# A sequence's routing laid out in six steps of a common clock instead of four, in a fused two-layer decoder kernel

## The chip, the cores and the metric

The kernel runs on one core of a Trainium2 chip. The metric is the device time of one execution in microseconds (us). Before the change it is 425.02 us, the median of 3 runs that lie between 424.5 and 425.11. The engines are named as in the profile: PE is the matrix engine (TensorE), PEld its weight loads, DVE the vector engine, ACT the scalar engine, POOL the GpSimd engine, SP the engine that here only issues DMAs.

## What is computed

The reference takes 4 sequences of 256 tokens of width 128 through two decoder layers. Each layer is self attention, cross attention and a mixture of 8 experts, with a layer norm behind each. The last of these, the second layer's mixture, sends every token to one expert with room for 128 tokens. What the change touches is how a token gets its place there (`_L1_ffn_ref`, cut):

```python
probs = jax.nn.softmax(xf.astype(jnp.float32) @ Wr, axis=-1)
eidx = jnp.argmax(probs, axis=-1)
p_tok = jnp.take_along_axis(probs, eidx[:, None], axis=1)[:, 0]
onehot = jax.nn.one_hot(eidx, E, dtype=jnp.int32)
rank_all = jnp.cumsum(onehot, axis=0) - onehot
rank = jnp.take_along_axis(rank_all, eidx[:, None], axis=1)[:, 0]
keep = rank < cap
slot = jnp.where(keep, rank, cap)
...
xe = xf[dispatch]
h = jnp.maximum(jnp.einsum('ecd,edf->ecf', xe, W1), 0.0)
ye = jnp.einsum('ecf,efd->ecd', h, W2)
```

## The kernel before, in words

Each engine has one program, written out in full before the launch. Its order comes from a clock that all engines' programs share: `by_the_clock` starts the stages (attention of a sequence, mixture, causal attention, routing) at given ticks and, in every tick, calls each live stage once, the one that started earliest first. What a stage emits in its step s stands in tick start + s, on every engine. Within an engine the instructions then run strictly in that order. Semaphores hold an instruction back until what it reads is there, and everything behind it on its engine waits too.

An attention takes 16 heads through these steps: from step 0 a head's scores by query go to a bank of pool D (L709) and DVE takes the row maxima (L1250, `negmax`); after each four heads two transposes (`shift`, L693) bring the maxima back and DVE adds them to the queries (L1245, `q_sp`); from step 8 a head's scores by key go to pool A (L720) and ACT takes exponentials (L997, `expo`); at steps 17 and 25 come the weighted values of eight heads each, into the one bank of pool C (L737, called pv below, `pair_done` at its end), which ACT copies out (L1003, `ctx_sb`). A mixture's products are L867 to L869 (up) and L851 (down), with DVE's L1309 behind each down product. Pool D has 4 banks and pool A 3. Banks are handed out in the order of the program, round the pool (`bank_turns`), so a product waits until the bank's last user has been read.

The routing of a sequence starts when its last attention (CROSS1) has ended, at ticks 175, 199, 223 and 239 for sequences 0 to 3. In the first three cases the attentions of later sequences are live; in the fourth nothing else is. In step 0 PE computes the logits (L919), and DVE copies them and makes the choice of the expert, the one-hot rows and their running count (L1366 to L1385, eleven small instructions, each linked to the next by a semaphore). In step 1 ACT takes the exponential (L1070) and DVE the sum (L1389 to L1391). In step 2 PE multiplies for the rank (L929, L931; needs `onehot_ready`) and DVE computes the slot (L1396 to L1404). POOL then writes the token rows to `xe_scratch` with two indirect DMAs (L515). For sequence 0 it also makes a table with an iota (L521). POOL's own list follows the order in which banks are handed out: the residual sum `xb` of an attention (L495) stands where its head 15 has its maxima, the scatter where the routing has its rank.

Before some of the last attention's products PE runs products that nobody reads (L629, `keep_busy`). After the routing of sequence 3 comes the second layer's mixture of all sequences (L1558 to L1586) and the output.

## Time and profile before

| | |
|---|---|
| median of 3 runs | 425.02 us |
| profiled execution, its own time | 425.88 us |
| span in that execution (first to last instruction) | 424.1 us |
| mean granted TensorE clock | 0.977 |
| PE busy / DVE / ACT / POOL | 377.5 / 284.7 / 226.1 / 54.4 us |
| routing of sequence 0, 1, 2, 3: logits copied by DVE at | 318.3, 350.8, 376.1, 391.8 us |

Times inside the execution count from the first instruction. Busy time says how long an engine worked, not whether anybody waited for it; for that one reads the rows in order of time, in which a bracket names the idle time of the engine before the instruction and what ended it. Matmuls overlap, so the start of the next one, not the printed end, shows when PE was ready for more.

### The profile page before, as it was taken

The page shows a single profiled execution, that of the slowest core. Times are in us where ns is not written, and L with a number is a line of the kernel's source. Part 1 is how long each engine was busy: PE and PEld are TensorE (multiplying, and loading weights), DVE is VectorE, ACT ScalarE, POOL GpSimd, SP SyncE. Part 2 cuts the span into 40 slices and gives each one's busy share as a digit, 9 for nine tenths or more (in the row PEclk, how much of TensorE's full clock was granted, in tenths as well). Part 3 has the DMA queues.
Part 4 walks back from the last instruction along what each step waited for, and adds up shares of the span by engine and source line. Part 5 has one row for each costly group of instructions (what it writes and reads, how often), then busy time and mean ns, then how long its engine had stood idle before and what let it go on. Part 6 is the DMA issues. An engine that isn't in the chain of part 4 may idle for free.

```text
span 424.1 us, 9115 instructions
## 1 busy us (share of the span) xinstructions
PE 377.5 (89%) x3274; PEld 331.8 (78%) x3274; DVE 284.7 (67%) x840; ACT 226.1 (53%) x526; POOL 54.4 (13%) x62
## 2 busy tenths in 40 slices
PE   4688898998989999999978999899999969979791
PEld 3576777886769997889967899878998757867691
DVE  6598889888965557722697264754668588853853
ACT  2145566665666564767337564585465635651241
POOL 7700004900000000000000000000003002010124
PEclk9989999999999999999979999999999989999997
DMA  5656310213340000200020000200003021652221
GB/s 157 197 160 191 113 52 26 75 47 90 123 145 2 2 2 0 76 2 2 2 68 8 2 0 2 56 21 1 2 5 85 5 71 39 204 169 63 55 69 34
DMA packets 23643, 25.68 MB, mean 61 GB/s; under 512 B 3240, under 2 KB 18353, under 8 KB 23600
## 3 DMA queue, kind: packets, MB, share of 16 engines
q1 hardware_dynamic: 22128, 23.47, 18.8%
q0 software_dynamic: 512, 0.97, 0.7%
q10 hardware_dynamic: 960, 0.66, 0.6%
q8 instruction: 27, 0.44, 0.4%
q14 instruction: 16, 0.13, 0.1%
HBM read 18.35 MB, written 6.83 MB: 59 GB/s over the span
## 4 chain that ended last, share of the span: by engine, by line
PE 68%; DVE 21%; issue 5%; ACT 3%; DMA 2%; POOLq 0%; SPq 0%; POOL 0%; ACTq 0%; DVEq 0%
PE bank_D L851 13%; PE bank_C L737 10%; PE bank_D L709 9%; PE bank_A L720 8%; DVE negmax L1250 5%; PE bank_A L867 4%; PE bank_A L869 3%; PE bank_A L868 3%; PE bank_D L635 2%; PE bank_D L693 2%; DVE x_rows L1182 1%; PE bank_D L768 1%; PE bank_A L655 1%; PE bank_A L1586 1%; PE bank_D L751 1%
## 5 line engine op out<-in xcount | busy, mean ns | idle before, releaser
L1250 DVE TENSOR_REDUCE negmax<-bank_D 128x2 f32<-128x512 f32 x192 | 127.6, 686 | 42.3 <-PE bank_D L709 41.8
L997 ACT ACTIVATE expo<-bank_A 128x512 f32<-128x512 f32 x192 | 110.2, 597 | 49.5 <-PE bank_A L720 47.2
L709 PE MATMUL bank_D<-k_head,q_sp 128*128 128x256 f32 x384 | 90.8, 321 | 9.6 <-DVE negmax L1250 4.7
L720 PE MATMUL bank_A<-q_sp,k_head 128*128 128x256 f32 x384 | 82.4, 300 | 4.9 <-DVE q_sp L1245 3.4
L1033 ACT ACTIVATE hidden<-bank_A,b 128x256 f32<-128x256 f32 x128 | 53.7, 471 | 52.1 <-PE bank_A L869 52.0
L709 PEld LDWEIGHTS bank_D<-k_head,q_sp 128*128 128x128 f32 x384 | 61.5, 199 | 21.9 <-issue 9.9
L851 PE MATMUL bank_D<-mix_w,hidden 128*128 128x128 f32 x512 | 67.8, 275 | 0.0
L720 PEld LDWEIGHTS bank_A<-q_sp,k_head 128*128 128x128 f32 x384 | 60.7, 194 | 7.7 <-DVE q_sp L1245 5.0
L851 PEld LDWEIGHTS bank_D<-mix_w,hidden 128*128 128x128 f32 x512 | 62.5, 191 | 1.6 <-issue 1.6
L737 PE MATMUL bank_C<-expo,v_aug 128*32 128x256 f32 x768 | 46.4, 382 | 1.1 <-ACT expo L997 0.5
L1309 DVE SCALAR_TENSOR_TENSOR y_mixture<-bank_D,g_w,y_mixture 128x128 f32<-128x128 f32 x64 | 22.3, 349 | 30.5 <-PE bank_D L851 28.8
L867 PE MATMUL bank_A<-x_hi,w_hi 128*128 128x256 f32 x128 | 41.2, 322 | 0.2 <-ACT hidden L1033 0.2
L495 POOL TENSOR_TENSOR xb<-x_rows,rows 128x256 f32<-128x256 f32 x12 | 8.3, 689 | 239.0 <-DVE y_attention L1230 237.4
L737 PEld LDWEIGHTS bank_C<-expo,v_aug 128*32 128x32 f32 x768 | 23.2, 109 | 16.2 <-issue 1.9
L869 PE MATMUL bank_A<-x_hi,w_lo 128*128 128x256 f32 x128 | 35.8, 279 | 0.0
L868 PE MATMUL bank_A<-x_lo,w_hi 128*128 128x256 f32 x128 | 35.7, 279 | 0.0
L1245 DVE TENSOR_TENSOR q_sp<-q_sp,bank_D 128x256 fp32r<-128x256 f32 x48 | 19.7, 410 | 8.6 <-PE bank_D L693 8.5
L867 PEld LDWEIGHTS bank_A<-x_hi,w_hi 128*128 128x128 f32 x128 | 24.3, 190 | 1.2 <-issue 0.7
L1003 ACT ACTIVATE ctx_sb<-bank_C 128x256 f32<-128x256 f32 x24 | 9.2, 385 | 28.2 <-PE bank_C L737 28.1
L868 PEld LDWEIGHTS bank_A<-x_lo,w_hi 128*128 128x128 f32 x128 | 24.3, 190 | 0.0
L869 PEld LDWEIGHTS bank_A<-x_hi,w_lo 128*128 128x128 f32 x128 | 24.1, 188 | 0.0
L515 POOL DMA_INDIRECT xe_scratch<-x_rows,slot x8 | 8.1, 1006 | 107.4 <-DVE slot L1404 106.2
(188 smaller groups left out, 529.9 us busy)
## 6 DMA issues: line engine op xcount, KB each, us to landing
mix_w<-in_mix_w SPq DMA_DIRECT2D x24, 256.0 KB, 3.5
k_head<-k_scratch SPq DMA_DIRECT2D x92, 48.0 KB
k_scratch<-qk_hi SPq DMA_DIRECT2D x24, 128.0 KB, 2.4
w_last<-in_mix_w SPq DMA_DIRECT2D x8, 256.0 KB, 6.3
k_scratch<-qk_lo SPq DMA_DIRECT2D x12, 128.0 KB, 2.3
proj_w<-in_proj SPq DMA_DIRECT2D x1, 640.0 KB, 5.7
xe_scratch<-empty_row SPq DMA_DIRECT2D x1, 520.0 KB, 4.5
expo<-xe_scratch SPq DMA_DIRECT2D x2, 260.0 KB, 3.2
```

What stands on the lines that cost most here:

```text
L709: last = mm(where(seq, b, ("max", k))[:, qt * SEQ:(qt + 1) * SEQ], q_sps[SET[seq, b]][:, k // 4, qt * P:(qt + 1) * P], k_heads[SET[seq, b] ...
L720: last = mm(where(seq, b, ("exp", h))[:, kt * SEQ:(kt + 1) * SEQ], k_heads[SET[seq, b]][:, t, g, kt * P:(kt + 1) * P], q_sps[SET[seq, b]][ ...
L737: last = mm(where(seq, b, ("pv", pair))[32 * g:32 * g + 32, 0:SEQ], v_augs[SET[seq, b]][:, kt, head(t, g), :], expo[:, exp_slot(seq, b, 4 ...
L851: last = mm(where(seq, b, ("down", e, qt))[:, 0:P], hidden[:, (e % 2) * FC + f, qt * P:(qt + 1) * P], mix_w2[:, e, f, :], start=(f == 0), ...
L867: mm(dst, w_hi, x_hi[:], start=True, stop=False)
L868: mm(dst, w_hi, x_lo[:], start=False, stop=False)
L869: last = mm(dst, w_lo, x_hi[:], start=False, stop=True)
L997: activate(expo[:, exp_slot(seq, b, h), :], where(seq, b, ("exp", h))[:], ACT.Exp, scale=float(HD) ** -0.5).then_inc(free(seq, b, ("exp", ...
L1033: last = activate(hidden[:, (e % 2) * FC + f, :], where(seq, b, ("up", n))[:, i * SEQ:(i + 1) * SEQ], ACT.Relu, bias=b1[:, e * FC + f:e * ...
L1245: V.tensor_tensor(q_sp[:, t, :], q_sp[:, t, :].bitcast(f32), where(seq, b, ("shift", t))[:, 0:SEQ], ALU.add).then_inc(free(seq, b, ("shift ...
L1250: V.tensor_reduce(negmaxes[SET[seq, b]][:, s // 4, :, 32 * (s % 4)], where(seq, b, ("max", s))[:].rearrange("p (q n) -> p q n", q=QT), AX. ...
L1309: V.scalar_tensor_tensor(y[b][:, qt, :], where(seq, b, ("down", e, qt))[:, 0:P], g_w[:, qt, e:e + 1], y[b][:, qt, :], ALU.mult, ALU.add).t ...
```

## The change

The routing gets six steps, with names. Logits on PE stay in step 0. DVE's choice moves from step 0 to step 1, ACT's exponential from 1 to 2, DVE's sum from 1 to 3, PE's rank product from 2 to 4, and DVE's slot from 2 to 5. No instruction is added or removed, and the starting ticks of all stages stay.

```diff
-ROUTE_STEPS = range(4)
+LOGITS_AT, FLAGS_AT, ROUTE_EXP_AT, TOTAL_AT, RANK_AT, SLOT_AT = 0, 1, 2, 3, 4, 5
+ROUTE_STEPS = range(SLOT_AT + 1)
...
     def routing(seq, b):
         for s in ROUTE_STEPS:
-            if s == 0:
+            if s == LOGITS_AT:
                 turn(seq, b, "logits", "D")
-            if s == 2:
+            if s == RANK_AT:
                 turn(seq, b, "rank", "D")
             yield
...
-                        if s == 2:
+                        if s == RANK_AT:
                             wait_free(pe, seq, b, "rank")
                             keep_busy(seq, b, where(seq, b, "rank"), "rank")
                             pe.wait_ge(onehot_ready, seq + 1)
...
-                        if s == 1:
+                        if s == ROUTE_EXP_AT:
                             act.wait_ge(shifted, seq + 1)
...
+                    for _ in range(FLAGS_AT):
+                        yield
+
                     wait_filled(dve, seq, ROUTE, "logits")
...
-                    yield
+                    for _ in range(FLAGS_AT, TOTAL_AT):
+                        yield
 
                     dve.wait_ge(routeexp_ready, seq + 1)
...
-                    yield
+                    for _ in range(TOTAL_AT, SLOT_AT):
+                        yield
```

The new lines shift the line numbers: PE's by 1, DVE's below the routing's choice by 4 to 6. In the rows below, L720 before is L721 of the change, L929 is L930, and so on.

Place 1 is the routing of sequence 0. This is PE's program there before the change, from the logits to pv of heads 0 to 7 of sequence 1:

```order
L919 MATMUL bank_D<-gate_w,xT_all 128x8 x2
L709 MATMUL bank_D<-k_head,q_sp 128x256 x2
L720 MATMUL bank_A<-q_sp,k_head 128x256 x2
L851 MATMUL bank_D<-mix_w,hidden 128x128 x4
L709 MATMUL bank_D<-k_head,q_sp 128x256 x2
L720 MATMUL bank_A<-q_sp,k_head 128x256 x2
L851 MATMUL bank_D<-mix_w,hidden 128x128 x4
L929 MATMUL bank_D<-onehot,const 128x8
L931 MATMUL bank_D<-before,const 128x8
L929 MATMUL bank_D<-onehot,const 128x8
L931 MATMUL bank_D<-before,const 128x8
```

And this is PE's program of the change, from the second of these two down products on, up to pv:

```order
L852 MATMUL bank_D<-mix_w,hidden 128x128 x4
L694 MATMUL bank_D<-const,negmax 128x128 x2
L710 MATMUL bank_D<-k_head,q_sp 128x256 x2
L721 MATMUL bank_A<-q_sp,k_head 128x256 x2
L852 MATMUL bank_D<-mix_w,hidden 128x128 x4
L710 MATMUL bank_D<-k_head,q_sp 128x256 x2
L721 MATMUL bank_A<-q_sp,k_head 128x256 x2
L930 MATMUL bank_D<-onehot,const 128x8
L932 MATMUL bank_D<-before,const 128x8
L930 MATMUL bank_D<-onehot,const 128x8
L932 MATMUL bank_D<-before,const 128x8
L721 MATMUL bank_A<-q_sp,k_head 128x256 x4
```

The rank's four products stood ahead of the shift (L693), head 14's scores, head 6's exponentials, a down product and heads 15 and 7; now they stand behind them, ahead of heads 8 and 9.

On DVE, at the same place, this stood between the end of the choice (L1385) and the slot before the change:

```order
L1385 TENSOR_REDUCE route_col<-route 128x2
L1250 TENSOR_REDUCE negmax<-bank_D 128x2
L1309 SCALAR_TENSOR_TENSOR y_mixture<-bank_D,g_w,y_mixture 128x128
L1389 TENSOR_REDUCE route_col<-route 128x2
L1390 RECIPROCAL x_rows<-route_col 128x2
L1391 COPY x_rows<-const 128x2
L1250 TENSOR_REDUCE negmax<-bank_D 128x2
L1309 SCALAR_TENSOR_TENSOR y_mixture<-bank_D,g_w,y_mixture 128x128
L1396 TENSOR_TENSOR route<-bank_D,onehot 128x16
```

In the change the choice ends with L1389, and this follows it:

```order
L1389 TENSOR_REDUCE route_col<-route 128x2
L1251 TENSOR_REDUCE negmax<-bank_D 128x2
L1310 SCALAR_TENSOR_TENSOR y_mixture<-bank_D,g_w,y_mixture 128x128
L1246 TENSOR_TENSOR q_sp<-q_sp,bank_D 128x256
L1251 TENSOR_REDUCE negmax<-bank_D 128x2
L1310 SCALAR_TENSOR_TENSOR y_mixture<-bank_D,g_w,y_mixture 128x128
L1394 TENSOR_REDUCE route_col<-route 128x2
L1395 RECIPROCAL x_rows<-route_col 128x2
L1396 COPY x_rows<-const 128x2
L1251 TENSOR_REDUCE negmax<-bank_D 128x2
L1168 BN_STATS stats_mixture<-y_mixture 128x6 x2
L1171 BN_AGGR mv_mixture<-stats_mixture 128x2 x2
```

One maximum (head 12) and one down product's sum that stood behind the choice now stand ahead of it, so what follows it is head 13 and the down product after.

Place 3 is the routing of sequence 2. PE's program there before, from the logits to the products that nobody reads ahead of the last pv:

```order
L919 MATMUL bank_D<-gate_w,xT_all 128x8 x2
L720 MATMUL bank_A<-q_sp,k_head 128x256 x4
L929 MATMUL bank_D<-onehot,const 128x8
L931 MATMUL bank_D<-before,const 128x8
L929 MATMUL bank_D<-onehot,const 128x8
L931 MATMUL bank_D<-before,const 128x8
L720 MATMUL bank_A<-q_sp,k_head 128x256 x4
L629 MATMUL bank_C<-proj_w 128x128 x4
```

And in the change:

```order
L920 MATMUL bank_D<-gate_w,xT_all 128x8 x2
L721 MATMUL bank_A<-q_sp,k_head 128x256 x8
L930 MATMUL bank_D<-onehot,const 128x8
L932 MATMUL bank_D<-before,const 128x8
L930 MATMUL bank_D<-onehot,const 128x8
L932 MATMUL bank_D<-before,const 128x8
L630 MATMUL bank_C<-proj_w 128x128 x4
```

The scores of heads 14 and 15 have moved from behind the rank to ahead of it. POOL's list changes at two places: the residual sums of sequence 1 and of sequence 2 stood behind the scatters of sequence 0 and of sequence 1, and now stand ahead of them. At the routing of sequence 3 every engine's order is the same as before.

## Rows read from the trace of the kernel before

**Rows 1.** The page: each engine's busy time, share and instructions.
```profile
PE 377.5 (89%) x3274; PEld 331.8 (78%) x3274; DVE 284.7 (67%) x840; ACT 226.1 (53%) x526; POOL 54.4 (13%) x62
```

**Rows 2.** PE in order of time, place 1: start, duration, instruction [idle before].
```profile
318.71 1.05 PE L851 MATMUL bank_D<-mix_w,hidden 128*128 128x128 f32 x8
320.08 1.05 PE L851 MATMUL bank_D<-mix_w,hidden 128*128 128x128 f32 x8
...
324.00 0.88 PE L720 MATMUL bank_A<-q_sp,k_head 128*128 128x256 f32 x6
325.18 1.93 PE L737 MATMUL bank_C<-expo,v_aug 128*32 128x256 f32 x32 [0.30 <-issue]
...
328.66 0.41 PE L779 MATMUL bank_A<-const,x_rows 128*128 128x128 f32 x2 [0.28 <-DVE x_rows L1182]
```

**Rows 3.** DVE in order of time, place 1.
```profile
318.33 0.18 DVE L1366 COPY route<-bank_D 128x16 f32<-128x16 f32 x1 [0.37 <-PE bank_D L919]
...
320.36 0.68 DVE L1250 TENSOR_REDUCE negmax<-bank_D 128x2 f32<-128x512 f32 x1
320.96 0.34 DVE L1309 SCALAR_TENSOR_TENSOR y_mixture<-bank_D,g_w,y_mixture 128x128 f32<-128x128 f32 x1
...
326.57 0.65 DVE L1179 SCALAR_TENSOR_TENSOR newton_mixture<-newton_mixture,r_mixture 128x2 f32<-128x2 f32 x1
327.25 0.62 DVE L1180 SCALAR_TENSOR_TENSOR newton_mixture<-newton_mixture,r_mixture 128x2 f32<-128x2 f32 x1
```

**Rows 4.** DVE's line L1179 over the whole execution: count, minimum, median, maximum ns.
```profile
L1179 DVE SCALAR_TENSOR_TENSOR newton_mixture<-newton_mixture,r_mixture x4: 160/163/646, 170.6 to 326.6; 128x2 f32<-128x2 f32 x4
```

**Rows 5.** POOL in order of time, scatters of sequences 0 to 2, the iota, a residual sum.
```profile
324.19 1.15 POOL L515 DMA_INDIRECT xe_scratch<-x_rows,slot  x1 [54.97 <-DVE slot L1404]
...
326.61 0.59 POOL L521 IOTA rope<- 128x512 f32 x1
327.14 0.71 POOL L495 TENSOR_TENSOR xb<-x_rows,rows 128x256 f32<-128x256 f32 x1
356.38 0.99 POOL L515 DMA_INDIRECT xe_scratch<-x_rows,slot  x1 [28.54 <-DVE slot L1404]
357.68 0.97 POOL L515 DMA_INDIRECT xe_scratch<-x_rows,slot  x1 [0.30 <-issue]
...
381.97 0.97 POOL L515 DMA_INDIRECT xe_scratch<-x_rows,slot  x1 [0.31 <-issue]
```

**Rows 6.** ACT in order of time, places 1 and 2.
```profile
327.17 0.39 ACT L1003 ACTIVATE ctx_sb<-bank_C 128x256 f32<-128x256 f32 x1 [0.41 <-PE bank_C L737]
...
330.31 0.38 ACT L966 ACTIVATE aT_causal<-bank_A 128x256 f32<-128x256 f32 x1 [0.28 <-PE bank_A L881]
...
359.24 0.38 ACT L1003 ACTIVATE ctx_sb<-bank_C 128x256 f32<-128x256 f32 x1 [1.68 <-PE bank_C L737]
```

**Rows 7.** PE in order of time, place 2 (the routing of sequence 1).
```profile
352.87 0.28 PE L929 MATMUL bank_D<-onehot,const 128*128 128x8 f32 x2
...
355.94 0.50 PE L720 MATMUL bank_A<-q_sp,k_head 128*128 128x256 f32 x2 [0.34 <-DVE q_sp L1245]
```

**Rows 8.** DVE in order of time, place 2, head 13's maxima.
```profile
354.11 0.69 DVE L1250 TENSOR_REDUCE negmax<-bank_D 128x2 f32<-128x512 f32 x1
```

**Rows 9.** PE in order of time, place 3 (the routing of sequence 2).
```profile
377.92 0.36 PE L929 MATMUL bank_D<-onehot,const 128*128 128x8 f32 x2 [1.31 <-DVE before L1377]
...
378.81 0.72 PE L720 MATMUL bank_A<-q_sp,k_head 128*128 128x256 f32 x4
379.37 1.05 PE L629 MATMUL bank_C<-proj_w 128*128 128x128 f32 x8
380.46 1.93 PE L737 MATMUL bank_C<-expo,v_aug 128*32 128x256 f32 x32
```

**Rows 10.** ACT in order of time, place 3.
```profile
379.32 1.08 ACT L997 ACTIVATE expo<-bank_A 128x512 f32<-128x512 f32 x2 [1.73 <-PE bank_A L720]
383.44 0.38 ACT L1003 ACTIVATE ctx_sb<-bank_C 128x256 f32<-128x256 f32 x1 [3.03 <-PE bank_C L737]
```

More of the change, by code:

```diff
@@ L913, in routing @@
                     for s in ROUTE_STEPS:
-                        if s == 0:
+                        if s == LOGITS_AT:
                             wait_free(pe, seq, b, "logits")
```

## The prediction, on record before the changed kernel ran

> **What bounds the kernel now.** I read the page's busy times first, then the three places of the routing engine by engine in order of time, then POOL. PE is busy for 377.5 us of the 424.1 us span, DVE for 284.7 [rows 1], so an instruction that PE cannot start is the thing to look for. No work is added or removed; only waits can change. So I ask at each place which wait PE has now and which it gets.
>
> At place 3 it has one that is plain to see: PE stood idle for 1.31 us in front of the rank's first product, until DVE had the running count, with heads 14 and 15 queued behind it [rows 9]. At place 2 PE did not wait for the rank's input; the wait it has comes later, 0.34 us in front of head 8's scores by key, which need DVE's `q_sp` [rows 7]. At place 1 PE runs from product to product; its first gap is the 0.30 us in front of pv, the next the 0.28 us in front of the mixture's transposes [rows 2]. Places 1 and 2 are therefore places where the change can cost as well as give. At the routing of sequence 3 no order changes, so nothing is expected from there.
>
> **Place 3, sequence 2.** Before, the order is rank, heads 14 and 15, the products nobody reads, pv. The wait ends at 377.92, and the rank's four products take until 378.81, 0.89 us. Heads 14 and 15 take from there to 379.37, 0.56 us; the unread products and pv follow, pv at 380.46 [rows 9]. In the change heads 14 and 15 run inside the wait: they fit, 0.56 against 1.31. DVE has nothing queued in ticks 223 and 224 but the choice, so the count is ready when it was, and the rank again starts at 377.92. The unread products follow at 378.81, and pv at 379.90. pv also needs the exponential of head 15, which before ended at 379.32 + 1.08 = 380.40, just as late as PE's own order [rows 10]. It moves with head 15's scores to about 378.7 by two exponentials behind each other, and is no longer last. Gain: 0.56 us. The bounds: nothing, if something other than PE's order sets when pv's result is out; and at most the whole wait, 1.31 us, if both parts count.
>
> There is a sign of such a thing. pv at 325.18 was copied out by ACT at 327.17, 1.99 us after its start; the pv at 380.46 was copied out at 383.44, 2.98 us after [rows 2, 6, 9, 10]. ACT was idle all that time. I see one thing that is special there: POOL's second scatter instruction, 381.97 to 382.94 [rows 5], runs across pv's end at 382.39. At place 1 the second one had ended at about 326.6, where the iota begins, before pv's end. This feeds two rivals below.
>
> **Place 2, sequence 1.** Now the choice moves behind head 12's maxima and the values' copies. Head 13's maxima began at 354.11, behind the choice, head 12, the copies and the sum [rows 8]; in the change the same stand ahead of them but for the sum (0.33 us), while the copies have to wait about as long for their product. I keep 354.1. The rank now stands behind heads 14, 6, 15 and 7 and takes the bank of head 13's maxima, so it waits until they are read: 354.11 + 0.60 (the step from one maxima to what follows, 320.36 to 320.96 [rows 3]) + 0.05, so 354.76. PE arrives at about 354.3, since the products from the shift to head 7 are five of 0.24 to 0.34 us behind 352.87, where the rank began before [rows 7]. The rank takes 0.89 [rows 9]; head 8 starts at 355.65 in place of 355.94, and its own wait is gone, since `q_sp` was read out by then. Gain: 0.3 us. Bounds: 0.86 if PE did not wait at all (the two delays in the stretch, 0.34 us of printed idle and about as much hidden by the overlap of matmuls, with the one ahead of head 15); a loss of 0.2 if head 13 is 0.5 later than I have it.
>
> **Place 1, sequence 0.** This is where the change costs. The choice takes 2.03 us of DVE, 318.33 to 320.36 [rows 3]. It moves behind head 12's maxima and a down product's sum. That down product began at 318.71 and ended at 319.76 [rows 2]; its sum takes DVE to about 320.06, and only then the choice starts: it ends at 322.09. Two things of PE wait for it. The next down product, before at 320.08 [rows 2], takes the bank of the logits, now read at 320.25: 0.2 us. The one after takes the bank of head 13's maxima, which start at 322.09 and free the bank 0.74 us later (320.36 to 321.10 was that distance for head 12): 322.83, while PE is there at 322.1. So 0.7 us of wait. Against this stands that the rank, 0.9 us, is no longer ahead of these products. Head 7's scores come at 323.96, as before at 324.00 [rows 2]. Then the rank, now behind head 7, takes 0.85, heads 8 and 9 0.5, and pv starts at 325.6 in place of 325.18: +0.43. Before, the rank's time had been covered by pv's wait for head 7's exponential.
>
> Behind pv part of it comes back. The transposes at 328.66 had waited for `x_rows` [rows 2]; DVE's Newton steps ahead of it took 0.65 and 0.62 us [rows 3] where the usual is 0.163 [rows 4]. They lie exactly under POOL's iota at 326.61 and its residual sum at 327.14 [rows 5]. In the change that sum stands ahead of the scatter and runs long before, and the scatter waits for the slot at about 326.6, so the iota comes at about 330, when DVE copies values out of a bank. The steps take 0.95 us less, but start 0.3 later, since ACT has head 8's exponential ahead of the root. `x_rows` is done at about 327.9, and PE is there last, at 328.5. ACT, which is 0.4 late with heads 10 and 11, has one gap to absorb it, the 0.28 us in front of the causal product's copy [rows 6]; its wait also shifts in part. I take a loss of 0.3 us for place 1. Bounds: 0 if the earlier transposes decide, 0.7 if DVE's waits are all paid.
>
> The Trainium skill, GPSIMD Engine Reference, section Key points, says that POOL shares its SBUF interfaces with DVE and contends with DVE instructions that have two SBUF inputs or run in a two-port mode. The Newton steps have two such inputs, and this trace agrees: 0.65 against 0.163 us. By that rule the iota's new place is harmless, and place 1 costs what I have; if the Newton steps stayed as slow, the transposes would come at 328.9 and place 1 would cost 0.2 more.
>
> **The sum** against the profiled execution's own 425.88 us: + 0.3 - 0.3 - 0.56 = -0.56, so 425.3. The median of the runs is 0.86 below that execution, so I give 425.02 - 0.56, about 424.4 us.
>
> **The rivals.** A measurement tells about 0.2% (0.85 us) from no change; the limits are 424.17 and 425.87.
>
> - A, the sum above: 424.4, with some 0.5 either way. Chance 0.36, of which a third lies under 424.17.
> - B, pv's result at place 3 is held by POOL's scatter and not by PE. The slot's time does not change there, so the scatter stays at 381.97, ACT copies at 383.44, and the 0.56 are lost: 425.0. For it: 2.98 against 1.99. Against: I know of no link between them. Chance 0.14.
> - C, the hold applies only when pv still runs under the second scatter instruction. pv now would end at 379.90 + 1.93 = 381.83, just ahead of 381.97. Then the copy comes 0.56 + 0.99 earlier: total -1.55, 423.5. Place 2's pv (357.68 to 358.65 under it, copied 2.4 us after its start at 356.84 by [rows 5, 6]) would lose its hold too, but PE and not ACT leads there. Chance 0.18.
> - D, slower: the hold moves to place 2. The slot there comes at about 357.3 instead of 355.5, so POOL starts at 358.15 (0.84 behind it, as the 356.38 was), and pv, from 356.5, ends at 358.4, under it. If the copy then waits until 0.5 us behind POOL's second instruction, at 361, instead of 359.24 [rows 6], ACT's exponentials of heads 10 and on stand still for 1.8 us and PE, with three banks of pool A, soon too. Price up to 1.8 + 0.3: 426.3. It decides when POOL's start falls ahead of pv's end, and I have 0.25 us of that. Against: place 1's POOL instructions delayed nothing. With it goes the plainer case of place 1 costing over 1.5. Chance 0.16.
> - E, the gains come back as waits between 360 and 372, where DVE and PE hand over to each other often, or in the stretch before the last layer: 425.0. Chance 0.08.
> - F, place 1 costs nothing: the earlier `x_rows` decides. 424.1. Chance 0.08.
>
> **How the numbers follow.** Faster by over 0.2%: C, F, and 0.14 of A, 0.40. Slower: D, 0.16. Within: the rest, 0.44. The range reaches from below C to over B and E, where it leaves out most of D and the lower tail of C: 423.2 to 425.7.
>
> **What would show it.** Right: at place 3 the idle time ahead of the rank's product is at most 0.6 us and pv starts 1.0 to 1.1 us behind the rank's end; at place 1 a down product waits some 0.7 us for DVE's maxima, pv starts 0.4 us later, and the Newton steps take 0.16 us; at place 2 the rank waits 0.4 us and head 8 does not. Wrong: place 3's copy of `ctx_sb` not moving with pv (B) or moving by 1.5 us (C); a `ctx_sb` at place 2 more than 2.5 us behind its pv (D). The prediction fails as a whole if DVE falls so far behind at place 1 that heads 14 and 15 wait as well, or if an order of DVE and POOL that I placed by hand comes out otherwise.

## The result and the profile after

The changed kernel is slower: 426.79 us median of 22 executions (423.82 to 428.22) beside 425.10 of the kernel before, ratio 1.0039 [1.0026, 1.0052]. The forecast was 424.4 us, with 425.7 as the upper end of its range. Two later comparisons of the same pair gave 0.9996 [0.998, 1.0012] and 1.0031 [1.0007, 1.0055]; the kernel's median was 426.17 and 426.44 us in them, so it is the kernel before that came out 0.9 us longer in the one that shows no difference. What has to be explained is the loss of 1.3 to 1.7 us in two of the three. The ratios here and below leave out an execution that is over 1.5% slower than the fastest of its kernel, such as the two of the kernel before at 430.1 and 430.5 us; they are not the quotients of the medians beside them and differ from these by up to 0.13%.

The profile does not show that loss at first sight. The execution that was profiled took 425.12 us, less than the 425.88 of the one shown for the kernel before, and every place that the prediction speaks of can be read in it. The page's span and its busy times, as in [rows 1]:

```profile
span 423.3 us, 9115 instructions
PE 378.8 (89%) x3274; PEld 332.5 (79%) x3274; DVE 284.2 (67%) x840; ACT 225.4 (53%) x526; POOL 54.4 (13%) x62
```

**Place 1.** PE of the changed kernel in order of time, in columns as in [rows 2]:

```profile
320.67 1.13 PE L852 MATMUL bank_D<-mix_w,hidden 128*128 128x128 f32 x8
...
323.21 1.13 PE L852 MATMUL bank_D<-mix_w,hidden 128*128 128x128 f32 x8 [0.72 <-DVE negmax L1251]
...
326.11 1.94 PE L738 MATMUL bank_C<-expo,v_aug 128*32 128x256 f32 x32
...
329.16 0.38 PE L780 MATMUL bank_A<-const,x_rows 128*128 128x128 f32 x2
```

DVE there, as in [rows 3], from the end of the sum that now stands ahead of the choice to the Newton steps:

```profile
320.36 0.16 DVE L1370 COPY route<-bank_D 128x16 f32<-128x16 f32 x1
...
322.38 0.68 DVE L1251 TENSOR_REDUCE negmax<-bank_D 128x2 f32<-128x512 f32 x1
...
327.29 0.16 DVE L1180 SCALAR_TENSOR_TENSOR newton_mixture<-newton_mixture,r_mixture 128x2 f32<-128x2 f32 x1
327.49 0.16 DVE L1181 SCALAR_TENSOR_TENSOR newton_mixture<-newton_mixture,r_mixture 128x2 f32<-128x2 f32 x1
```

POOL's first scatter and its iota there, which were at 324.19 and 326.61 in [rows 5]:

```profile
328.01 1.15 POOL L516 DMA_INDIRECT xe_scratch<-x_rows,slot  x1 [21.73 <-DVE slot L1410]
...
330.42 0.60 POOL L522 IOTA rope<- 128x512 f32 x1
```

**Place 2.** PE, as in [rows 7]: the rank now waits, head 8 behind it does not.

```profile
355.76 0.39 PE L930 MATMUL bank_D<-onehot,const 128*128 128x8 f32 x2 [0.67 <-DVE negmax L1251]
...
356.67 0.48 PE L721 MATMUL bank_A<-q_sp,k_head 128*128 128x256 f32 x2
...
357.55 1.93 PE L738 MATMUL bank_C<-expo,v_aug 128*32 128x256 f32 x32
```

**Place 3.** PE, as in [rows 9]:

```profile
378.59 0.36 PE L930 MATMUL bank_D<-onehot,const 128*128 128x8 f32 x2 [0.35 <-DVE before L1381]
...
379.48 1.14 PE L630 MATMUL bank_C<-proj_w 128*128 128x128 f32 x8
380.55 1.93 PE L738 MATMUL bank_C<-expo,v_aug 128*32 128x256 f32 x32
```

and ACT's copy of what pv made, as in [rows 10]:

```profile
382.55 0.38 ACT L1004 ACTIVATE ctx_sb<-bank_C 128x256 f32<-128x256 f32 x1 [3.30 <-PE bank_C L738]
```

The 1.31 us ahead of the rank have become 0.35, and the copy starts 2.00 us behind pv where it had been 2.98.

To measure a place, I take the starts of ACT's copies (`ctx_sb`, `xT_all`) in the traces of two kernels and subtract. Ahead of place 1 the changed kernel stood 0.29 us behind the profiled execution of before (copy at 313.71 there), behind place 1 0.83 (335.40), behind place 2 0.68 (374.57), and at place 3's copy it was 0.89 ahead (383.44). So the places cost +0.54, -0.15 and -1.57 us, -1.2 in sum. By the second trace of the kernel before, further down, 1.0 of the -1.57 belongs to a copy that came late in that one profiled execution, which leaves place 3 -0.6 and the sum -0.2. A kernel that loses in its median what its profiled execution gains calls for the other executions: of the 22, nine are above 427 us, at a mean granted clock of 0.971 or 0.972, and the profiled one, at 0.979, is not of them.

### The profile page after: what moved, and what is told of

Same layout as the page of the kernel before. It is cut to its first block, busy times and chain, and to the rows that moved or that the text cites. A ratio compares the mean times of both kernels' runs of the same rounds, so it can differ in the third digit from the quotient of the medians.

```text
span 423.3 us, 9115 instructions
## 1 busy us (share of the span) xinstructions
PE 378.8 (89%) x3274; PEld 332.5 (79%) x3274; DVE 284.2 (67%) x840; ACT 225.4 (53%) x526; POOL 54.4 (13%) x62
## 4 chain that ended last, share of the span: by engine, by line
PE 70%; DVE 19%; issue 5%; ACT 3%; DMA 1%; ACTq 0%; POOLq 0%; SPq 0%; POOL 0%; DVEq 0%
PE bank_D L852 13%; PE bank_C L738 10%; PE bank_D L710 9%; PE bank_A L721 8%; DVE negmax L1251 5%; PE bank_A L868 4%; PE bank_A L870 3%; PE bank_A L869 3%; PE bank_D L636 2%; PE bank_D L694 2%; DVE x_rows L1183 1%; PE bank_D L769 1%; PE bank_A L656 1%; PE bank_A L1592 1%; PE bank_D L752 1%
## 5 line engine op out<-in xcount | busy, mean ns | idle before, releaser
L721 PE MATMUL bank_A<-q_sp,k_head 128*128 128x256 f32 x384 | 82.9, 301 | 4.5 <-DVE q_sp L1246 3.1
L721 PEld LDWEIGHTS bank_A<-q_sp,k_head 128*128 128x128 f32 x384 | 60.8, 194 | 7.5 <-DVE q_sp L1246 4.5
L694 PE MATMUL bank_D<-const,negmax 128*128 128x128 f32 x96 | 19.4, 285 | 0.6 <-DVE negmax L1251 0.4
```

Of the source, the lines that this page charges most:

```text
L694: last = nc.tensor.transpose(where(seq, b, ("shift", t))[:, qt * P:(qt + 1) * P], negmaxes[SET[seq, b]][:, t, qt, :], ident)
L721: last = mm(where(seq, b, ("exp", h))[:, kt * SEQ:(kt + 1) * SEQ], k_heads[SET[seq, b]][:, t, g, kt * P:(kt + 1) * P], q_sps[SET[seq, b]][ ...
```

## The experiments

Two devices serve all of them. `FILL` puts products that nobody reads, of the kind of `keep_busy`, into waits that PE has anyway:

```
+FILL = {(3, CAUSAL1, "turn"): 6, (1, CROSS1, "turn"): 4, (2, ROUTE, "rank"): 5}
...
+                    for _ in range(FILL.get((seq, b, what), 0)):
+                        mm(dst[:, 0:P], weight("ov"), weight("ov"), start=True, stop=True)
```

The first two entries (below "near 345") lie ahead of the two pairs of transposes of `x_rows` for which PE waits 1.47 and 0.75 us there, the third ahead of the rank of sequence 2, at place 3. A table gives each sequence its own steps:

```
+ROUTE_AT = [(0, 1, 2, 3, 4, 5), (0, 0, 1, 1, 2, 2), (0, 0, 1, 1, 2, 2), (0, 0, 1, 1, 2, 2)]
...
-            if s == 0:
+            if s == ROUTE_AT[seq][0]:
...
-            if s == 2:
+            if s == ROUTE_AT[seq][4]:
```

Row 0 above has the six steps, the others the four of before. The results, each beside the kernel before on the same chip (12 executions each, 23 to 35 of the kernel before):

| kernel | median us | before | ratio | above 427 us |
|---|---|---|---|---|
| changed, again | 426.17 | 425.95 | 0.9996 [0.998, 1.0012] | 2 of 12 |
| six steps at place 1 alone | 427.44 | 425.95 | 1.0022 [1.0007, 1.0036] | 7 of 12 |
| at place 2 alone | 424.92 | 425.95 | 0.9982 [0.9969, 0.9995] | none |
| at place 3 alone | 425.34 | 425.95 | 0.9978 [0.9962, 0.9995] | 1 of 12 |
| before + five products at place 3 | 424.45 | 425.06 | 0.9987 [0.9967, 1.0006] | none |
| before + ten near 345 | 426.27 | 425.06 | 1.0016 [0.9991, 1.0042] | 2 of 12 |
| before + both | 423.21 | 425.06 | 0.9965 [0.9938, 0.9992] | none |
| changed + ten near 345, one at place 3 | 423.07 | 425.06 | 0.9947 [0.993, 0.9965] | none |
| place 1 alone + five at place 3 | 425.70 | 425.03 | 1.0012 [0.9996, 1.0027] | none |
| before + two at place 1 | 425.83 | 425.03 | 1.0006 [0.9988, 1.0023] | none |
| places 2 and 3 alone + ten, one | 423.23 | 425.03 | 0.9964 [0.9943, 0.9984] | none |
| changed, again | 426.44 | 425.03 | 1.0031 [1.0007, 1.0055] | 5 of 12 |
| changed + ten near 345 | 422.75 | 424.58 | 0.9964 [0.9943, 0.9984] | none |
| changed + one at place 3 | 425.12 | 424.58 | 1.0026 [1.0008, 1.0045] | 2 of 12 |

The kernel before itself was above 427 us in 6 of 127 executions in these four batches, and in 8 of all its 151.

### One place at a time

The changed kernel once more, and three kernels with a `ROUTE_AT` that has the six steps in one row only.

> The changed kernel as it is, once more, for a second profile and more times. Its first profiled execution took 425.12 us with a mean granted clock of 0.979, faster than the profiled execution of before (425.88), while the median of its 22 runs is 426.79 and most of the slower ones show a mean clock of 0.967 to 0.971. Theory T (the order alone sets the time, the prediction's bookkeeping): the times gather at 425.1 and the rest is chance; the new median is within 0.5 us of that of before. Theory C (clock): in most executions TensorE is granted its lower level for a further stretch that the first profile did not catch; the median is again 1.2 to 2.2 us above that of before, and a profile of over 426.5 us shows the lower level in a stretch where the first one does not.

> Six steps for sequence 0 alone, the old four for the others. Theory T: in the profile of the change everything from the transposes on was later by about 0.5 us at place 1, so the median is 0.3 to 0.7 us above that of before and the mean clock is that of before, 0.977. Theory C, with the cause at place 1 (the gap that it opens in PE's work, or the shift by half a microsecond of what follows): median 1.5 us or more above, mean clock 0.971 or less.

> Six steps for sequence 1 alone. Theory T: place 2 gave 0.15 us in the profile of the change, median 0 to 0.4 us below that of before, mean clock as before. Theory C with the cause at place 2 (a longer wait of PE ahead of the rank's product, 0.67 us in the profile): median 1.5 us or more above, mean clock lower by 0.005 or more, with the lower level somewhere between 350 and 375 us.

> Six steps for sequence 2 alone. Theory T: place 3 gave 0.6 us up to pv and a further 1.0 where pv's result is copied out, so the median is 0.5 to 1.6 us below that of before. Theory C with the cause at place 3: median 1 us or more above that of before, with the lower level in the tail behind 380 us.

In the traces the places add up: place 1 alone cost +0.53 us at its place, place 2 alone -0.17, place 3 alone -0.64. The times of all executions do not: by the medians place 2 alone is 1.0 us below the kernel before and place 3 alone 0.6, and place 1 alone is 1.5 above (by the ratios 0.8, 0.9 and 0.9 us), about two to three times what its place costs. The changed kernel itself was meant to separate two theories and did not: its median is 0.2 us above, as Theory T has it, and its profiled execution, 425.92 us, has a further stretch at the lower clock behind 378 us, as Theory C has it; it is in the table of seven traces further down. The profiled execution of place 1 alone (427.88 us) shows where the rest is. PE's rank and pv at place 3 and ACT's copy, in order of time:

```profile
379.08 0.36 PE L930 MATMUL bank_D<-onehot,const 128*128 128x8 f32 x2 [1.30 <-DVE before L1381]
...
381.63 3.49 PE L738 MATMUL bank_C<-expo,v_aug 128*32 128x256 f32 x32
...
385.19 0.38 ACT L1004 ACTIVATE ctx_sb<-bank_C 128x256 f32<-128x256 f32 x1 [3.62 <-PE bank_C L738]
```

and the same stretch by windows (busy time and count of PE, PEld, DVE, ACT, POOL, then the granted clock, the DMA share and GB/s):

```profile
380.00:382.00 2.00, 1.98 (x18) 1.59 (x21) 0.73 (x5) 1.08 (x2) 0.17 (x1) 0.85 0.01 2
382.00:384.00 2.00, 2.00 (x24) 0.98 (x20) 0.00 (x0) 0.00 (x0) 1.70 (x2) 0.50 0.09 32
384.00:386.00 2.00, 2.00 (x20) 1.16 (x13) 0.00 (x0) 0.38 (x1) 0.10 (x1) 0.79 0.09 31
```

The 32 products of pv take 3.49 us where they take 1.93 at full clock: TensorE is granted 0.50, its level of 1.2 GHz, through nearly all of them. Nothing at the place of the change shows this; it is 55 us behind it. Four of the seven executions of place 1 alone above 427 us, this one among them, have a mean granted clock of 0.976.

### The waits filled

If it is the lower level that makes the difference, filling the waits ahead of it should take it away, at no cost of time while the products stay inside the wait.

> The kernel before, with five products that nobody reads in PE's 1.31 us wait ahead of the rank's product of sequence 2 (they take 0.227 us each, so 1.13 us). Single profiles so far show three lengths from pv's start at place 3 to the copy of its result: 2.0 us, 2.7 to 3.0 us, and 3.6 us where the profile shows TensorE at its lower level there. Theory C (the idle and nearly empty stretch ahead of it brings a stretch at the lower level in some executions): the copy comes 2.0 us behind pv's start, and the median falls by 0.5 to 1.5 us. Theory H (POOL's scatter holds pv's end): the scatter is where it was, the copy stays 2.7 to 3.0 us behind pv's start, and the median moves by less than 0.3 us.

> The kernel before, with six and four products that nobody reads in PE's waits ahead of the two transposes at 345.44 and 346.61 us, behind which every profile so far shows the lower level for 3 to 6 us. Theory C: that stretch goes away or gets short, the mean clock rises to 0.98 or more, and the median falls by 0.5 to 1.5 us. If the waits are not the cause: mean clock and median as before, within 0.3 us.

> Both fillings in the kernel before. Theory C: the sum of the two, 1 to 3 us below the kernel before, and the runs lie closer together than 1 us from the second lowest to the second highest.

> The changed kernel with the same filling in the middle and one such product (0.227 us) in the 0.35 us wait that is left at place 3. With the clock's part gone, the order's own part should stand alone. Theory T (place 1 costs 0.53, place 2 gives 0.15, place 3 gives 0.6 as the profiles show): 0.1 to 0.4 us faster than the kernel before with both fillings. If place 1 costs more than its profile shows: slower than it by 0.5 us or more.

With five products at place 3 the kernel before has this on PE, POOL and ACT, in order of time:

```profile
380.65 1.93 PE L740 MATMUL bank_C<-expo,v_aug 128*32 128x256 f32 x32
380.86 0.99 POOL L516 DMA_INDIRECT xe_scratch<-x_rows,slot  x1 [9.19 <-DVE slot L1407]
382.15 0.98 POOL L516 DMA_INDIRECT xe_scratch<-x_rows,slot  x1 [0.30 <-issue]
...
382.65 0.38 ACT L1006 ACTIVATE ctx_sb<-bank_C 128x256 f32<-128x256 f32 x1 [2.05 <-PE bank_C L740]
```

The second scatter runs from 382.15 to 383.13, across pv's end at 382.58, as in [rows 5], and yet the copy starts 2.00 us behind pv and not 2.98. So a second scatter across pv's end is not enough to hold its result. A later profile of the kernel before, unchanged, says the same: pv at 381.03, copy at 383.03, with the second scatter from 382.53. It is not needed either. With place 3 alone:

```profile
380.66 1.93 PE L738 MATMUL bank_C<-expo,v_aug 128*32 128x256 f32 x32
382.75 0.98 POOL L516 DMA_INDIRECT xe_scratch<-x_rows,slot  x1 [0.30 <-issue]
...
383.59 0.38 ACT L1004 ACTIVATE ctx_sb<-bank_C 128x256 f32<-128x256 f32 x1 [4.22 <-PE bank_C L738]
```

The copy is 2.93 us behind pv at full clock, with a scatter that starts behind pv's end. So the late copy is not a property of one execution: it is there at place 3 in three of the 20 traces (the first of before, place 2 alone 3.04 us, place 3 alone) and, with 2.4 to 2.5 us, at place 2 in three (the first of before, place 1 alone, place 3 alone); every other pv that ran at full clock is copied out after 2.0 us. It belongs neither to the old order nor to the new one, and what makes it stays open. The median of the five products at place 3 is 0.6 us below that of the kernel before, as Theory C has it, but the interval of its ratio holds no change as well.

Ten products near 345 alone did not lower the median of the kernel before (426.27), against what was expected. Its profiled execution, 422.40 us, has no stretch of lower level between 340 and 400 us; but others of its twelve were at 426.5 to 426.9, at 429.7 and at 429.8 us. Both fills together brought 423.21, and for the changed kernel 423.07. Between these last two the places differ by +0.54, -0.17 and -0.57 us in the traces, -0.20 in sum, and the medians by -0.14. That agrees, but it proves little: the two ratios are 0.18% apart, 0.8 us, and their intervals overlap. Nor are the executions of the old order with both fills as close together as expected (less than 1 us from the second lowest to the second highest): these are 422.64 and 426.10 us, beside 422.41 and 423.69 for the changed kernel. What is plain is that each kernel with both fills is 1.5 to 2.3 us below the kernel before, whichever order it has.

### Place 1 again, and a plain shift

> Six steps for the routing of sequence 0 alone, as in the run that came out 1.5 us (0.22%) over the run with the old steps, plus five products that nobody reads in the wait ahead of the rank product of sequence 2. Theory T (at place 1 the new order costs its 0.54 us and no more; the rest of the 1.5 us is TensorE granted its lower level around the weighted values of the last place, which those five products prevent): the copy ctx_sb of place 3 ends 2.0 to 2.1 us behind the weighted values where it ended 3.56 us behind, the granted clock of 378 to 386 us stays near 1.0, and the median is about 0.5 us over the old order with the same five products (which measured -0.13% against the kernel before): -0.1 to +0.1% against the kernel before. Rival K (place 1 itself costs 1.5 us in most executions, by something that the one profiled does not show): the median stays 0.2 to 0.35% over the kernel before, with the tail as short.

> The old order, and at place 1 alone two products that nobody reads, some 0.45 us of TensorE's time, ahead of the rank product of sequence 0. Theory T' (any delay of about 0.5 us at place 1 moves what follows so that TensorE meets its lower level more often or for longer further down): the median is 1 to 1.5 us over the kernel before (+0.2 to +0.35%), as with six steps at place 1. Rival S (a delay costs its own length at most, and what six steps at place 1 cost over 0.54 us has to do with the order of the instructions there): 0 to +0.5 us, at most +0.12%.

> Six steps for the routings of sequences 1 and 2, the old four for sequence 0, and unread products in the two waits (six and four near 345 us, one ahead of the rank product of sequence 2). Theory T (the terms of the order add up: place 1 +0.54, place 2 -0.17, place 3 -0.59): 0.5 us under the changed kernel with the same products, which measured 0.53% under the kernel before: -0.5 to -0.8%, near 422.5 us when the kernel before is at 425.1. Rival K (place 1 costs 1.5 us): -0.8 to -1.0%. If the size of the clock's stretches is drawn anew whenever anything moves, the result can lie anywhere from -0.3 to -0.8%.

> The changed kernel as it is, once more beside the kernel before. It was +0.39% the first time and -0.04% the second. Theory T (order -0.2 us in sum, the rest is which stretches of lower level an execution meets): between -0.1 and +0.4%, with a spread of its executions of over 2 us, and the executions of 1 us and more over the fastest at a lower mean granted clock. Rival (a fixed cost of 1.7 us in the order): +0.3 to +0.5% again.

The five products at place 3 take the seven executions above 427 us away from place 1 alone, and the copy is 2.00 us behind pv in the trace (381.81 and 379.81), as Theory T has it. The ratio, 1.0012 [0.9996, 1.0027], is a little above what T expected, and its interval reaches into K's range, so it does not exclude K by itself; against the old order with the same five products it is 1.1 us by the two ratios, where T had 0.5. That seven executions above 427 us became none does speak against K, and so do the traces further down, in which place 1 costs the same whatever the execution takes. The plain shift is not settled: two products at place 1 moved what follows by 0.25 us only, not 0.45, its interval spans both theories, and none of its executions is above 427 us. Its profiled execution, 425.82 us, has in the old order what the slower traces of the changed kernel have (the table below): a long stretch at the lower level from 344.5 us and a further one from 378.6. These two are not made by the new order alone, then, and not every execution that has them is above 427 us. Places 2 and 3 with the waits filled (423.23) are no faster than the changed kernel with them filled, measured in another batch, so the 0.54 us of place 1 did not come back as a whole; at -0.36% the result is outside the ranges of both T and K and inside the one given for stretches that fall anew whenever anything moves. In its profiled execution, 422.85 us, it did (place 1 +0.01); its other executions decide the median.

### Which wait, and which executions

> The changed kernel, with the six and four unread products in the waits near 345 us and nothing at the last place. With both fills it had measured 0.53% under the kernel before, all of its executions within 422.3 to 423.8 us; unfilled it measured +0.39, -0.04 and +0.31%, with a third of its executions and more above 427 us. Theory M (the executions above 427 us are those in which the stretch of lower level near 344 to 350 us is followed by one near 378 to 384 us, and the first is what these ten products take away): no execution above 426 us, median near 423.3 us, ratio -0.3 to -0.6%. Rival N (the last place alone decides, by the single product in its wait): the group above 427 us stays, ratio -0.1 to +0.3%.

> The changed kernel with one unread product, 0.2 us, in the 0.35 us wait ahead of the rank product of sequence 2 and nothing near 345 us. Theory M: little changes, ratio 0 to +0.4%, and executions above 427 us are still there. Rival N: the group above 427 us is gone and the ratio is -0.3 to 0%, as five such products took it away from the kernel with six steps at place 1 alone.

> The changed kernel, for one more profile. The three profiles so far are all of executions with a mean granted clock of 0.978 and 425 to 426 us; about half of its executions have 0.971 and 427 to 428 us. Should this one be of those, Theory M expects a second stretch of lower level behind 378 us as in the kernel with six steps at place 1 alone (weighted values 3.4 us, copy ctx_sb 3.5 us behind them), with nothing at place 1 itself; rival K expects the missing 2 us at place 1, between 313 and 336 us.

> The same once more, for the same reason: a mean granted clock of 0.971 goes with 2 us that lie behind 378 us (Theory M) or between 313 and 336 us (rival K).

> The kernel before, for a second profile of it. Theory M expects of its order what it says of the changed one: where the stretch of lower level near 344 us is a long one (6.8 us) that begins behind 344.3 us, another follows near 378 us and the execution is near 426 us or above; where it is short and begins at 346 us or later, none follows and the time is 424 to 425.5 us.

> The changed kernel for one more profile. Theory M: with a mean granted clock of 0.978 and no stretch behind 378 us about 425 us, with one there 426 us; at 0.971 near 427.5 us, and then the 2 us lie behind 344 us in two long stretches, not at place 1.

Ten products near 345 take the changed kernel to 422.75 us, with one execution of twelve above 424.2; one product at place 3 leaves it at +0.26%, with executions at 427.3 and 427.5. Theory M holds in this, with one execution at 426.18 where it allowed none above 426, and N falls. The single profiled executions give most of what was missing: two are of 426.73 and 427.08 us, with a mean granted clock of 0.967. None is of 0.971, so of the main group above 427 us there is no trace. First the changed kernel's profiled execution of 425.12 us:

```profile
344.00:346.00 2.00, 0.81 (x6) 0.60 (x6) 1.89 (x7) 1.12 (x3) 0.00 (x0) 1.00 0.44 117
346.00:348.00 2.00, 0.98 (x5) 0.80 (x6) 1.89 (x8) 0.38 (x1) 0.00 (x0) 0.78 0.13 27
348.00:350.00 2.00, 2.00 (x10) 1.85 (x8) 1.54 (x3) 0.97 (x2) 0.00 (x0) 0.50 0.00 0
350.00:352.00 2.00, 2.00 (x15) 1.82 (x14) 1.30 (x3) 1.13 (x4) 0.00 (x0) 0.86 0.00 0
...
380.00:382.00 2.00, 2.00 (x34) 1.36 (x36) 0.43 (x4) 0.00 (x0) 0.66 (x1) 1.00 0.03 4
382.00:384.00 2.00, 2.00 (x26) 1.59 (x15) 0.18 (x1) 0.38 (x1) 1.31 (x2) 1.00 0.09 32
```

and then the same program in another execution, 427.08 us:

```profile
344.00:346.00 2.00, 0.53 (x3) 0.20 (x2) 1.79 (x10) 0.74 (x2) 0.00 (x0) 0.95 0.37 100
346.00:348.00 2.00, 1.29 (x7) 1.30 (x7) 1.86 (x5) 0.77 (x2) 0.00 (x0) 0.50 0.00 0
348.00:350.00 2.00, 2.00 (x10) 1.82 (x9) 0.99 (x3) 0.98 (x2) 0.00 (x0) 0.50 0.00 0
350.00:352.00 2.00, 2.00 (x11) 2.00 (x11) 1.32 (x3) 0.60 (x1) 0.00 (x0) 0.50 0.00 0
352.00:354.00 2.00, 2.00 (x17) 2.00 (x15) 1.36 (x7) 1.24 (x3) 0.00 (x0) 0.84 0.00 0
...
380.00:382.00 2.00, 2.00 (x12) 1.70 (x16) 0.74 (x5) 0.00 (x0) 0.30 (x1) 0.50 0.03 4
382.00:384.00 2.00, 2.00 (x28) 0.95 (x24) 0.00 (x0) 0.00 (x0) 1.65 (x2) 0.66 0.09 32
```

The figure behind the five busy times, the granted clock, is the one to read. In the first execution the stretch at the lower level near 347 us is short: the shares missing from 1.00 are 0.22, 0.50 and 0.14 of 2 us each, at half clock, so it is 2 x 0.86 x 2 = 3.4 us long. There is none at 380 us. In the second it begins at 345.8 us in place of 347.1 and is twice as long, and a further one lies at 380 us, where the products that nobody reads and pv take 1.96 and 2.71 us in place of 1.14 and 1.93:

```profile
379.83 1.96 PE L630 MATMUL bank_C<-proj_w 128*128 128x128 f32 x8
381.72 2.71 PE L738 MATMUL bank_C<-expo,v_aug 128*32 128x256 f32 x32
```

What PE did before the clock fell is alike in both: it waited ahead of the transposes, 1.47 us ahead of the first pair in the one and in the other. In the first execution:

```profile
346.27 0.41 PE L780 MATMUL bank_A<-const,x_rows 128*128 128x128 f32 x2 [1.47 <-DVE x_rows L1183]
347.43 0.66 PE L780 MATMUL bank_A<-const,x_rows 128*128 128x128 f32 x2 [0.75 <-DVE x_rows L1183]
```

Seven traces are of the changed kernel as it is or with its one product. The numbers between are differences of ACT's copies against the profiled execution of before, as in the section on the result: at its place 1 (313.71 to 335.40), and over the two stretches that follow:

| execution, us | place 1 | 335.40 to 374.57 | 374.57 to 383.44 | lower level near 347 / 380 |
|---|---|---|---|---|
| 425.12 | +0.54 | -0.15 | -1.57 | short / none |
| 425.14 (one product) | +0.53 | -0.32 | -1.64 | short / none |
| 425.43 | +0.53 | -0.19 | -1.58 | short / none |
| 425.92 | +0.53 | +0.67 | +0.21 | long / yes |
| 426.25 | +0.52 | +0.63 | +0.02 | long / yes |
| 426.73 | +0.53 | +0.97 | +0.05 | long / yes |
| 427.08 | +0.55 | +0.91 | +0.03 | long / yes |

Place 1 is the same to 0.03 us in all. The long stretch costs 0.8 to 1.3 us over the short one, and the one at 380 us 1.6 to 1.9 us: 2.4 to 3.0 us in sum between two executions of one program, over ten times the sum of the places. The times at the left differ by less, because at 313.71, ahead of place 1, the four with the long stretch stood 0.7 to 2.0 us earlier than the other three; that difference arises in the first 35 us (0.3 to 1.5 us) and near 220 us, where further stretches of the lower level lie that differ too, ahead of anything that the change touches. From this an estimate for the group without a trace: the execution of 425.12 us with both later stretches in place of its short one would take 2.4 to 3.0 us more, 427.5 to 428.1, with 6.8 us more at half clock, which lowers its mean clock from 0.979 to 0.971. The nine above 427 us lie between 427.09 and 428.22 at 0.971 or 0.972. Both traces of the kernel before, at 425.88 and 425.59 us, have the short stretch and none at 380; with the plain shift its order has both, and with five products at place 3 the long one alone. That the long stretch need not bring the other is seen at place 3 alone (426.01 us), where it began at 344.0 us and 378 to 384 us had 1.00; and at place 1 alone the short one was followed by one at 381 us.

The stretches also change what the order costs. The plain shift (old order, 425.82 us) and the changed kernel at 425.92 us can be laid side by side: the copies at 335.40 are 0.02 us apart in them, and the long stretch begins at 344.5 in one and 344.3 in the other. At place 2 the plain shift has

```profile
350.08 0.17 DVE L1369 COPY route<-bank_D 128x16 f32<-128x16 f32 x1
...
356.17 1.93 PE L740 MATMUL bank_C<-expo,v_aug 128*32 128x256 f32 x32
```

and the changed kernel

```profile
352.15 0.17 DVE L1370 COPY route<-bank_D 128x16 f32<-128x16 f32 x1
...
354.91 0.39 PE L930 MATMUL bank_D<-onehot,const 128*128 128x8 f32 x2 [0.67 <-DVE negmax L1251]
...
356.71 1.93 PE L738 MATMUL bank_C<-expo,v_aug 128*32 128x256 f32 x32
```

In the old order DVE makes the choice from 350.08 on, while PE is still slow; in the new one it waits for PE (0.69 and 0.32 us), begins the choice at 352.15, behind the values' copies, and PE at full clock then waits for DVE. Place 2, a gain of 0.15 us behind the short stretch, is a loss of 0.5 behind the long one (+0.66 beside +0.15 from 335.40 to 374.57). From 313.71 to 383.44 the new order costs 0.5 to 0.8 us in executions with both stretches, the 0.25 of the shift taken off, where its sum is -0.2 without them. This rests on one trace of the old order (425.82) and two of the new (425.92 and 426.25).

With ten products near 345 the changed kernel has no stretch there:

```profile
344.00:346.00 2.00, 1.96 (x18) 1.77 (x17) 1.86 (x8) 1.03 (x2) 0.00 (x0) 1.00 0.40 120
346.00:348.00 2.00, 2.00 (x19) 1.98 (x18) 1.93 (x7) 0.77 (x2) 0.00 (x0) 1.00 0.00 1
348.00:350.00 2.00, 1.91 (x16) 1.65 (x14) 2.00 (x6) 1.55 (x4) 0.00 (x0) 1.00 0.00 0
```

It is 1.56 us faster than the kernel before's profiled execution from 335.40 to 374.57 and 1.57 from there to 383.44. This version, the change with ten more products, beats the kernel before: 0.9964 [0.9943, 0.9984]; with one product more at place 3, 0.9947 [0.993, 0.9965]; and so does the old order with both fills, 0.9965 [0.9938, 0.9992]. The three intervals overlap, so the gain is shown for the fills and not for the order.

## Why the prediction was wrong

**Place 1, +0.3 forecast, +0.54 measured.** The mechanism was right in its steps: PE waits 0.72 us (0.7 forecast) for head 13's maxima, the choice starts at 320.36 (320.06 by my working, in an execution that stood 0.29 behind), pv comes 0.93 us later, or 0.64 less the offset (0.43 forecast), and the Newton steps take 0.16 us each. The Trainium skill, GPSIMD Engine Reference, section Key points, has the contention of POOL and DVE that I used for them; the trace agrees, 0.65 and 0.62 us under the iota and the residual sum before, 0.16 and 0.16 without them after. What was mis-sized is what comes back behind pv: the transposes no longer wait, but PE reaches them 0.50 us later (0.21 without the offset, where I had it 0.16 earlier), and ACT's copies behind them are 0.53 and 0.54 late.

**Place 2, -0.3 forecast, -0.15 measured.** The rank waits 0.67 us, not 0.4, since it stands on DVE's maxima; head 8's wait is gone, as forecast. Where the long stretch lies ahead of it the place costs 0.5 instead; the prediction reckoned it at full clock only.

**Place 3, -0.56 forecast, -0.6 by its order.** Heads 14 and 15 run inside the wait, and pv starts 1.96 us behind the rank's start where it had been 2.54. Place 3 alone measured -0.64. The further 1.0 us in the first pair of profiles is the copy's 2.98 us, which a second execution of the kernel before does not have and two of other versions do; so rivals B, C and D, with 0.48 of the chance, most of it built on that row, had no hold by the scatter behind them. A row that is odd in one execution is not yet a wait of the program.

**The sum.** -0.56 was forecast; the order gives +0.54 - 0.15 - 0.6 = -0.2, and the two kernels with both waits filled differ by -0.14 in their medians, which are not known that closely.

**The step that failed** is the last one, "the median of the runs is 0.86 below that execution, so I give 425.02 - 0.56". It takes the executions as one distribution that moves as a whole with the sum of the places. They are not: which stretches of lower level one meets is worth 2.4 to 3.0 us. In the changed kernel 17 of its 49 executions are above 427 us, in the kernel before 8 of 151. That it is the new order at place 1 that brings them is shown (7 of 12 with it alone, 1 of 24 with place 2 or 3 alone), and that filling the waits near 345 us takes them away in the changed kernel is shown too (none of 24 with ten products there). That they meet the lower level behind 340 us is seen at place 1 alone and estimated for the changed kernel, from its slower traces. Why the new order brings them is argued and not shown: 0.54 us of delay moves the waits near 345 us, and what PE does at 378 us, against the moments at which the clock falls, which themselves lie up to 3 us apart from execution to execution; part of the slower median may also be the 0.5 us that place 2 loses behind a long stretch. The plain shift of 0.25 us did not bring the group, so a size of delay from which it comes, or some part that the order itself has in it, stays open. So does why ten products near 345 us without the order of place 3 left the kernel before at 426.27: there PE's wait of 1.31 us ahead of the rank is still unfilled, and I have no trace of one of its slower executions.

None of the rivals was this. D had its sign, and nothing of its cause.

## What to carry to other kernels

Before a change of a few tenths of a microsecond is weighed, take several profiles of one and the same kernel and compare the granted clock by windows: where stretches at the lower level differ between them, they are worth more than the change, and the waits just ahead of them are the thing to work on first. Filling such a wait with products that nobody reads was worth 1.5 to 2.3 us against the kernel before in four versions here, but filling one wait of two left the kernel before where it was, or worse (426.27 beside 425.06): measure the fills, too, by many executions. A gain in one place can turn into a loss when the clock ahead of it is slow. And where a profiled execution says faster and the median says slower, look for the group of executions that was not profiled before changing the theory of the place.

## What the runs showed that I had not expected

One program, on one chip, had its lower stretch near 345 us begin at 344.3 or at 347.4 us and last 3.4 or 6.8 us, with the same wait of 1.47 us of PE beside its start. The Trainium skill, TensorE: Matmul & The Clock Gate, Part 1, says of a kernel's start that the number of products at the lower level is "run-variable"; these traces agree, and show it in the middle of a kernel, 345 and 380 us from its start, too.

A wait of 0.35 us ahead of the rank, in place of 1.31, did not keep the clock up at 378 to 383 us: four of the six executions above that have it fell to 0.50. Ten products 33 us ahead of it did, in the execution that was profiled.
